# First group's q by four fp32 products of the loaded weight and x, in place of twelve of their split halves

## What is computed

```python
def _L0(x, adj, ...):                       # attention, 8 heads of 32, masks for each head
    q = split_heads(x @ Wq.T + bq)
    k = split_heads(x @ Wk.T + bk)
    v = split_heads(x @ Wv.T + bv)
    scores = einsum('bhsd,bhtd->bhst', q, k) * SCALE
    scores = where(mask, scores, -1e9)      # 6 static masks, 2 of adj | eye
    out = softmax(scores) @ v
    return out @ Wo.T + bo

def _L1(h, adj, W, bW, attn, A_w, fc_w, g1_w, g2_w, gbias):   # 4 heads
    Wh = einsum('bni,hoi->bhno', h, W) + bW
    e = einsum('bhno,hop->bhnp', Wh, attn)
    A_mat = tanh(where(adj, einsum('bhnp,bhmp->bhnm', e, Wh), 0))
    hp = relu(einsum('bhnm,bhmo->bhno', A_mat, Wh))
    ...                                     # ha, hf, a sigmoid gate between them

x = layernorm(x + _L0(x, adj, ...))
x = layernorm(x + _L1(x, adj, ...))
```

## Time and profile before

| | us |
|---|---|
| median of 3 runs | 1094.99 |
| lowest and highest | 1093.66, 1097.73 |
| the profiled execution | 1096.53 |
| its span | 1094.4 |
| PE busy in the span | 1079.4 (99%) |
| DVE, ACT, POOL busy | 732.6, 531.4, 284.1 |

### The profile page before, as it was taken

How to read it: one execution, slowest core, us unless ns; L and a number is a source line. 1 busy time by engine, 2 the same in 40 slices (tenths; PEclk the granted TensorE clock), 3 DMA queues, 4 the chain that set the end, 5 groups by cost and what they waited for, 6 DMA issues and landing times.

```text
span 1094.4 us, 25365 instructions
## 1 busy us (share of the span) xinstructions
PE 1079.4 (99%) x10090; PEld 905.4 (83%) x10090; DVE 732.6 (67%) x1379; ACT 531.4 (49%) x947; POOL 284.1 (26%) x249
## 2 busy tenths in 40 slices
PE   8999999999999999999999999999999999999997
PEld 6888788888888888788888888888888888888886
DVE  7785766767677585765757667585775757667545
ACT  5663453635446363563635446363563635536351
POOL 1542231231322213222231312213222232312200
PEclk9999999999999999999999999999999999999999
DMA  7000100100010000100100010000100001010000
GB/s 263 2 25 19 41 24 27 34 20 19 22 40 22 20 19 22 40 22 20 41 19 21 22 40 22 20 19 22 40 22 20 31 13 37 22 41 3 1 20 20
DMA packets 26860, 32.59 MB, mean 30 GB/s; under 512 B 4432, under 2 KB 23376, under 8 KB 26448
## 3 DMA queue, kind: packets, MB, share of 16 engines
q1 hardware_dynamic: 26400, 31.93, 8.7%
q10 hardware_dynamic: 432, 0.26, 0.1%
HBM read 23.80 MB, written 8.39 MB: 29 GB/s over the span
## 4 chain that ended last, share of the span: by engine, by line
PE 97%; DVE 2%; DMA 1%; issue 0%; POOL 0%; ACT 0%; DVEq 0%
PE bank L389 18%; PE bank L390 17%; PE bank L394 17%; PE bank L381 8%; PE bank L383 8%; PE bank L382 8%; PE bank L602 5%; PE bank L625 4%; PE bank L529 2%; PE bank L516 2%; PE bank L547 2%; PE bank L572 1%; PE bank L709 1%; PE bank L429 0%; DMA raw_q<-in_wq 0%
## 5 line engine op out<-in xcount | busy, mean ns | idle before, releaser
L920 ACT ACTIVATE cat_hi<-bank 128x512 fp32r<-128x512 f32 x128 | 76.6, 598 | 128.5 <-PE bank L394 128.5
L885 ACT ACTIVATE T<-bank 128x512 f32<-128x512 f32 x128 | 75.8, 594 | 78.4 <-PE bank L394 78.1
L1034 DVE SCALAR_TENSOR_TENSOR cat_lo<-bank,cat_hi 128x512 fp32r<-128x512 f32 x128 | 86.5, 685 | 40.6 <-ACT cat_hi L920 39.7
L389 PE MATMUL bank<-hT_hi,g_lo 128*128 128x512 f32 x256 | 102.7, 401 | 0.0
L383 PE MATMUL bank<-cat_hi,aw_hi 128*128 128x512 f32 (+1 forms) x272 | 102.4, 377 | 0.0
L382 PE MATMUL bank<-cat_hi,aw_lo 128*128 128x512 f32 (+1 forms) x272 | 102.4, 377 | 0.0
L381 PE MATMUL bank<-cat_lo,aw_hi 128*128 128x512 f32 (+1 forms) x272 | 102.4, 377 | 0.0
L1386 POOL TENSOR_TENSOR probs<-probs,den 128x512 f32<-128x512 f32 x64 | 67.1, 1059 | 131.5 <-DVE den L1125 131.5
L390 PE MATMUL bank<-hT_hi,g_hi 128*128 128x512 f32 x256 | 99.9, 390 | 0.0
L390 PE MATMUL bank<-U_hi,wt_hi 128*128 128x512 f32 x256 | 99.8, 390 | 0.0
L389 PE MATMUL bank<-U_hi,wt_lo 128*128 128x512 f32 x256 | 99.8, 390 | 0.0
(11 more groups left out here) (183 smaller groups left out, 2768.9 us busy)
## 6 DMA issues: line engine op xcount, KB each, us to landing
y<-in_x SPq DMA_DIRECT2D x16, 512.0 KB, 3.4
out<-res SPq DMA_DIRECT2D x15, 512.0 KB, 3.0
x_raw<-in_xT SPq DMA_DIRECT2D x14, 512.0 KB, 3.3
W_nat<-in_Wn SPq DMA_DIRECT2D x1, 1028.0 KB, 7.7
attn_nat<-in_attn SPq DMA_DIRECT2D x1, 1024.0 KB, 9.9
adjS_u<-in_adjS SPq DMA_DIRECT2D x32, 32.0 KB, 2.7
raw_A<-in_AwT SPq DMA_DIRECT2D x1, 1024.0 KB, 8.7
x_second<-in_xT SPq DMA_DIRECT2D x1, 512.0 KB, 10.1
```

Of the source, the lines that this page charges most:

```text
L389: pe.matmul(out, wsel(w[1]), dsel(d[0]), start=first and n == 0, stop=False)
L885: take(act.activation(T[:, n % DC, n // DC, :], bank[:], ACT.Copy), "B", f"T{n}", g)
L920: act.activation(cat_hi[:, n, :], bank[:], ACT.Relu).then_inc(cat_hi_ready, 1)
L1034: return dve.scalar_tensor_tensor(out=out, in0=bank, scalar=bias, in1=hi.bitcast(F32), op0=op, op1=ALU.subtract)
```

## The change

In `first_queries` the twelve products of split halves become four plain fp32 products of `raw_q` and `x_raw`, the tiles as they were loaded. The order is turned too: input chunk k is the outer loop and output chunk c the inner one, with both banks claimed ahead. PE waits for the transfers themselves (`early_in[0]`, `first_in`, then `xT_in`) and not for the splits. The splits are still made, since `Wq`'s are needed by the 15 other groups and `x_hi` and `x_lo` by this group's keys and values. `keys(0)` gets the wait for `x_ready` that `first_queries` had. `second_load`, which overwrites `raw_q`, waits until both banks of q have been evicted.

```diff
@@ second_load (SP)
                 sp.wait_ge(weights_ready, 2)
+                for c in range(DC):
+                    await_taken(sp, "A", f"q{c}", 0)
                 load(x_second[:], xT[1:2].rearrange("o p c t -> (o p) c t"), xT_in)
@@ first_queries (PE)
-                for c in range(DC):
-                    bank = claim(pe, "A", f"q{c}", 0)
-                    cols = slice(c * P, c * P + P)
-                    for k in range(DC):
-                        if c == 0:
-                            pe.wait_ge((first_hi, x_hi_ready)[k], 1)
-                            if k == 0:
-                                pe.wait_ge(early_hi, 1)
-                        pe.matmul(bank[:], Wq[0][:, k, cols], x_hi[:, k, :], start=k == 0, stop=False)
-                        if c == 0 and k == 0:
-                            pe.wait_ge(weights_ready, 1)
-                        pe.matmul(bank[:], Wq[1][:, k, cols], x_hi[:, k, :], start=False, stop=False)
-                    if c == 0:
-                        pe.wait_ge(x_ready, 1)
-                    for k in range(DC):
-                        ins = pe.matmul(bank[:], Wq[0][:, k, cols], x_lo[:, k, :], start=False, stop=k == DC - 1)
-                    filled(ins, "A", f"q{c}", 0)
+                pe.wait_ge(early_in[0], 16)
+                banks = [claim(pe, "A", f"q{c}", 0) for c in range(DC)]
+                for k in range(DC):
+                    pe.wait_ge((first_in, xT_in)[k], 16)
+                    for c in range(DC):
+                        ins = pe.matmul(banks[c][:], raw_q[:, k, c * P:c * P + P], x_raw[:, k, :], start=k == 0, stop=k == DC - 1)
+                        if k == DC - 1:
+                            filled(ins, "A", f"q{c}", 0)
@@ keys (PE)
                     pe.wait_ge(weights_ready, 2)
+                    pe.wait_ge(x_ready, 1)
```

## The result

The changed kernel took 1099.18 us (median of 8, 1098.77 to 1100.28), the kernel before 1095.23 (median of 8, 1093.66 to 1097.83). The ratio is 1.0036, with a 95% interval of 1.0027 to 1.0045. The forecast was 1094.6 with a range of 1092.8 to 1097.4: the change makes the kernel 3.95 us slower, where I expected it 0.4 faster, and the time lies outside the range. It stays within the 0.5% that I called no change.

The account below looks back on a forecast made before the run. PE was taken to bound the kernel, with waits only in the first 30 us. Keys 0.6 us earlier, limited by `W_nat` to 0.38, gave 1094.99 - 0.38 = 1094.6 us, range 1092.8 to 1097.4.

Parts of the forecast that it names:

- The price of a product: First group's q on PE: each plain fp32 product of 512 columns takes 0.85 us, four take 3.41.
- The start of q at 5.4 to 5.6: Start-up on PE: q products start when the warm-up lets them, so the keys start 0.6 us earlier.
- rival 3: Start-up: PE at 1.2 GHz during all four q products, keys 2.9 us later, 1097.9 us; chance 0.04.
- The cap by `W_nat`: Near 15 us: DVE's shift of `W_nat` until 14.66 limits the 0.6 gain to 0.38 at the softmax's first add.
- rival 1: Near 15 us: `W_nat` lands before 9.85 in most executions, the whole 0.6 or 0.77 arrives, 1094.3 us; chance 0.05.
- What reaches the end: After start-up: the change only shifts everything behind it; DVE's 0.38 us gain passes to PE and the end.
- SP's added wait: `x_second` on SP, issued at 13.45: the added wait is over 3 us earlier and costs nothing.
- The range: Whole kernel: 1092.8 to 1097.4 us, from three executions of the kernel before at 1093.66 to 1097.73.

Follow-up runs that it names:

- a1: The changed kernel, unchanged, run once for a second trace: 1096.10 us, the kernel before 1094.73.
- a3: The changed kernel, unchanged, timed once more beside two others on one chip: median 1098.82 us, ratio 1.0026 to the kernel before.
- b_short_pad8: The kernel before with the first group's q from hi x hi products alone and sixteen already met waits added: 1097.74 us, ratio 1.0026.
- a_pad7_again: The changed kernel with fourteen already met waits (seven instructions) ahead of the keys, timed again: 1095.03 us, ratio 1.0001 to the kernel before.
- a2: The changed kernel, unchanged, timed in ten executions beside its variants: median 1097.65 us, ratio 1.0016 to the kernel before.
- b_short: The kernel before with the first group's q from hi x hi products alone, every wait kept: 1098.48 us, ratio 1.0027.
- a_pad15_again: The changed kernel with thirty already met waits (fifteen instructions) ahead of the keys, timed again: 1094.40 us, ratio 0.9994 to the kernel before.
- a_wu2: The changed kernel with two warm-up products in place of three and 34 already met waits: 1093.48 us, ratio 0.9985 to the kernel before.

## Why the prediction was wrong, step by step

- **The price of a product**, 0.85: right. The halves stand 0.43 apart once the clock is up (7.09, 7.52).
- **The start of q at 5.4 to 5.6**: right for an early rise of the clock (5.59 in a1), wrong for a late one (6.59 in the profile after). I took the rise at 4.0 to 4.6 from one execution as a property of the kernel. By each trace's own record of the clock it came anywhere from 4.1 to 7.5 in sixteen traces (4.2 in the profile before, 6.7 in that after). The 1.00 that the windows give at 6 to 7 us was no evidence for it: they give 1.00 at 3 to 4 us too, in the profile before and in that after, where the halves stand 0.85 apart. The Trainium skill ("TensorE: Matmul & The Clock Gate", Part 1) says that it moves; I cited that, in rival 3, and gave it 0.04. But my rival asked for the whole of q at half the clock (+2.9). What happens is a part of it, often: with three warm-ups and a rise at 6.0 or later the scores began 0.2 to 0.95 later than at 13.49.
- **The cap by `W_nat`**: right where `W_nat` is as late as in the earlier trace rows or later. In a1 the 0.50 at the scores becomes 0.14 at `M1`, which then waits for DVE, and 0.34 further on. In a3 it lands earlier and all of the 0.5 arrives. The condition of rival 1, `W_nat` before 9.85 in most executions, held in twelve of sixteen traces, where I had given it 0.05.
- **What reaches the end**: this is the step that failed, and it cost most of the 3.95 us. "Whatever it does there reaches the end as a shift of everything behind it, and no further." The change also shortened PE's program by seven instructions, and this changed when its blocks were fetched. b_short_pad8 (1.0026, without a plain fp32 product) and a_pad7_again (1.0001, with them and the seven instructions put back) show it from both sides. I checked every queue for the wait that was added and never asked what the instructions that were gone did to the supply of the others, though PE's waits had a line "issue", 1.8 us, in the scores. In the lined-up profiles the idle time that this made in the second scores is 2.0 of the 2.3 us, and the late clock at the start 0.6. By medians the seven instructions are worth 2.4 to 3.8.
- **SP's added wait** cost nothing: `x_second` was issued at 13.32 in the profile after, 13.45 before.
- **The range** rested on the spread of the kernel before, as if the changed one must have the same. Its own, in the ten executions of a2, is 5 us.

What stays open is why the packet comes late. Counting PE's records when it is fetched, the one that PE ran out for in the second scores was at the 933rd to 952nd in all ten traces with the count of before or more, and at the 937th, 968th, 970th, 1120th, 1140th and 1141st in the six with 7 or 15 fewer. Only the last three made PE stand still there; in those at 968 and 970, a1 and b_short_pad8, the next block's first record came 2.75 and 2.59 us after the packet, so these passed by little. The end of the stretch, the 1217th record, lies in the second scores in all of them, so it isn't the place where PE runs out that the seven instructions move out of the way, but the moment of the request; what triggers it no view shows.

## What to carry to other kernels

Taking instructions out of a long program isn't neutral: look for idle time with "issue" as its releaser in loops of small instructions, and for the packets of the instruction queue beside it. Before an edit that ought to change little is judged by its time, measure it at several positions, by adding instructions that do nothing, and set it against the kernel before at the same position. A single execution's clock, at the start above all, is no property of the kernel.

## What the runs showed of the hardware that I had not expected

- PE stood still for 0.7 to 2.7 us where its next 16 KB of instructions came late: before the program's repeated turns always after the 705th, 1217th or 2497th record, and once more near 978 us. It went on 2.3 to 2.9 us after the start of the packet, in all 23 cases.
- After idle times of 1.98 us (a3), 2.30 and 1.89 us (b_short) the granted clock fell to 0.50 within 1.5 us of PE's going on and stayed there for 3 to 4 us, which cost 1.6 us in a3. After one of 2.65 us in a_pad15_again it did not fall.
- Fourteen or thirty waits that are already met, 7 or 15 instructions, cost PE nothing that the times show. The traces of a_wu2 and b_short_pad8 have 0.15 us of idle time ahead of the keys, with "issue" as its releaser.
